# Linear attention beside a routed feed-forward layer: expert rows transposed on VectorE instead of TensorE, and three weight buffers

## The reference

```
xn  = layernorm(x)                        # x: [1, 1024, 256]
out = x + attention(xn) + ffn(xn)

attention: q, k, v = split(xn @ w_qkv);  q, k = elu(.) + 1;  16 heads of 16 columns
           s_t  = decay * s_{t-1} + k_t          # scan over the 1024 tokens
           kv_t = decay * kv_{t-1} + k_t * v_t
           (q * kv / max(sum_head(q * s), 1e-6)) @ w_out
ffn:       e(t), score(t) = the best of 8 experts by xn @ router_w.T
           routed = (silu(g) * u) @ w_down[e],   g, u = split(xn * sigmoid(score) @ w_gate_up[e])
           shared = (silu(g) * u) @ shared_down, g, u = split(xn @ shared_gate_up)
```

## Time and profile before

| | |
|---|---|
| median of 3 runs | 128.91 us (128.76 to 129.81) |
| the profiled execution's own time | 129.24 us |
| its span | 127.6 us |
| TensorE busy | 122.1 us (96%), clock granted in full |
| VectorE, ScalarE, GpSimd busy | 79.4 (62%), 53.4 (42%), 35.4 us (28%) |
| moved by DMA | 25.02 MB, mean 196 GB/s |

### The profile page before, as it was taken

How to read it: one execution, slowest core, us unless ns; L and a number is a source line. 1 busy time by engine, 2 the same in 40 slices (tenths; PEclk the granted TensorE clock), 3 DMA queues, 4 the chain that set the end, 5 groups by cost and what they waited for, 6 DMA issues and landing times.

```text
span 127.6 us, 2426 instructions
## 1 busy us (share of the span) xinstructions
PE 122.1 (96%) x822; PEld 106.1 (83%) x822; DVE 79.4 (62%) x175; ACT 53.4 (42%) x113; POOL 35.4 (28%) x65
## 2 busy tenths in 40 slices
PE   4989999999999999999999999999999999999990
PEld 1248776788888857999999999999999978999990
DVE  0799695997899999875575553505040428922471
ACT  1678796829987546322222222242221337200000
POOL 7804040003879300040303030303030301687500
PEclk9999999999999999999999999999999999999999
DMA  3784999999993210129797989888982031033437
GB/s 83 207 281 37 330 360 244 181 207 397 385 380 136 82 51 0 46 81 318 264 321 258 295 275 277 307 280 303 281 303 63 9 86 51 13 89 104 112 101 244
DMA packets 15748, 25.02 MB, mean 196 GB/s; under 512 B 1296, under 2 KB 12632, under 8 KB 15736
## 3 DMA queue, kind: packets, MB, share of 16 engines
q1 hardware_dynamic: 13368, 20.66, 53.1%
q0 software_dynamic: 1456, 3.41, 8.2%
q10 hardware_dynamic: 912, 0.80, 1.9%
HBM read 18.78 MB, written 6.08 MB: 195 GB/s over the span
## 4 chain that ended last, share of the span: by engine, by line
PE 80%; POOL 6%; issue 5%; DMA 4%; DVE 2%; ACT 0%; DVEq 0%; POOLq 0%
PE ps L1112 25%; PE ps L1126 13%; PE ps L300 6%; POOL q_sb L458 6%; PE ps L302 5%; PE ps L301 5%; PE ps L975 5%; PE ps L988 4%; PE ps L981 4%; PE ps L1066 4%; DMA q_sb<-sorted_rows,slot_row 2%; PE ps L1053 2%; DMA sorted_rows<-yrow 2%; PE ps L1060 2%; DVE x_sb L895 1%
## 5 line engine op out<-in xcount | busy, mean ns | idle before, releaser
L1112 PE MATMUL ps<-xgT,gu 128*128 128x144 f32 x256 | 34.2, 287 | 0.0
L1112 PEld LDWEIGHTS ps<-xgT,gu 128*128 128x128 f32 x256 | 32.3, 190 | 0.5 <-issue 0.2
L826 DVE TENSOR_TENSOR wqkv<-rz,ps 128x288 f32<-128x288 f32 x16 | 7.3, 454 | 25.5 <-ACT rz L576 25.5
L440 POOL DMA_DIRECT2D sorted_rows<-yrow x9 | 5.0, 558 | 54.7 <-DVE yrow L821 54.7
L1126 PE MATMUL ps<-wqkv,dn 128*128 128x144 f32 x128 | 17.4, 289 | 0.0
L576 ACT ACTIVATE rz<-ps 128x288 f32<-128x288 f32 x16 | 6.5, 409 | 25.0 <-PE ps L1112 25.0
L1126 PEld LDWEIGHTS ps<-wqkv,dn 128*128 128x128 f32 x128 | 16.1, 190 | 0.0
L432 POOL DMA_INDIRECT sorted_rows<-xn,slot_row x8 | 9.8, 1220 | 15.4 <-ACT xn L514 13.6
L300 PE MATMUL ps<-xT_hi,sgu_hi 128*128 128x512 f32 x32 | 13.0, 407 | 0.0
L301 PE MATMUL ps<-xT_lo,sgu_hi 128*128 128x512 f32 x32 | 12.6, 394 | 0.0
L302 PE MATMUL ps<-xT_hi,sgu_lo 128*128 128x512 f32 x32 | 12.6, 394 | 0.0
(11 more groups left out here) (162 smaller groups left out, 231.3 us busy)
## 6 DMA issues: line engine op xcount, KB each, us to landing
gu<-in_L_ffn_w_gate_up_dram SPq DMA_DIRECT2D x8, 1024.0 KB
dn<-in_L_ffn_w_down_dram SPq DMA_DIRECT2D x8, 512.0 KB
sorted_rows<-zeros SPq DMA_DIRECT2D x1, 2592.0 KB, 18.0
wqkv<-sorted_rows SPq DMA_DIRECT2D x10, 144.0 KB
sorted_rows<-yrow POOLq DMA_DIRECT2D x9, 128.0 KB, 2.1
sgu<-_ffn_shared_gate_up_dram SPq DMA_DIRECT2D x1, 1024.0 KB, 6.2
wqkv<-in_L_attn_w_qkv_dram SPq DMA_DIRECT2D x3, 256.0 KB, 3.7
x_sb<-in_L_attn_x_dram SPq DMA_DIRECT2D x2, 256.0 KB, 3.6
```

What stands on the lines that cost most here:

```text
L826: V.tensor_tensor(hr[:, 2 * h:2 * h + 2, :].rearrange("p f s -> p (f s)"), act_sb[:, h, 0:2 * SLOTS], ps[:, 2 * h + 1, 0:2 * SLOTS], ALU.m ...
L1112: ins = mm(ps[:, 2 * h + u, (f % 2) * SLOTS:(f % 2 + 1) * SLOTS], gu[p][:, kc, col:col + P], xgT[:, kc, :], start=(kc == 0), stop=(kc == K ...
```

## The change

- **Rows in.** The four DMAs of a new `sorted_load` each bring 32 partitions of `xg`: partition q*32 + p holds, for each of 5 blocks of 32 rows, 64 columns of row p of the block (256 bytes). One VectorE `transpose` of 32x32 blocks (`sorted_in`) makes `xgT` from it; TensorE's and ScalarE's part in this goes away. Features then lie in another order over the partitions, so `gu` is loaded as "(p c)" instead of "(c p)".
- **Results out.** `rows_out` transposes the down result from PSUM to `yrow` in one VectorE instruction; four DMAs store it, in the same pieces of 256 bytes, from SyncE's queue instead of GpSimd's. `yrow` has one buffer. For this order the down product takes every second column of `dn` as its weights. The last group's stores are issued two by SyncE and two by ScalarE.
- **Three weight buffers.** The third lies in `xT_raw` and `ez`, which are free once the routing and the q, k, v products are done. Expert 2 is loaded before the loop, and expert e + 3 after expert e.
- **Three parts.** Gate/up goes in parts of 2, 1 and 1 hidden blocks of 128 columns. The third part uses banks 4 and 7, which the transposes used before.
- **VectorE's list.** The first two `kv_scan` move from before the loop to after the first pass, the other two to after the second; the products with q move to after the fifth.

```diff
-        xg = early[0:HS, 0:2 * D].rearrange("p (j d) -> p j d", j=2)
+        gu_of = [gu[0][:, :, :], gu[1][:, :, :], xT_raw[:, :, :]]
+        dn_of = [dn[0][:, :, :], dn[1][:, :, :], ez[:, :, :].rearrange("p b t -> p (b t)").rearrange("p (f d) -> p f d", f=FC)]
+        xg = early[:, 0:NSQ * SQ * KC].rearrange("p (j f) -> p j f", j=NSQ)
...
-        gu_dram = w_gate_up.rearrange("e (c p) n -> e p c n", p=P)
+        gu_dram = w_gate_up.rearrange("e (p c) n -> e p c n", c=KC)
...
+        GATE = (0, 2, 4)
+        UP = (1, 3, 7)
+        PARTS = ((0, 1), (2,), (3,))
...
+        def row_store(eng, t, q, s_store):
+            rows = sorted_rows[bass.ds(t * SLOTS, NSQ * SQ), q * SQ * KC:(q + 1) * SQ * KC]
+            eng.dma_start(rows.rearrange("(j p) f -> p j f", p=SQ), yrow[q * SQ:(q + 1) * SQ, :, :]).then_inc(s_store, 16)
...
 # SyncE
+            def sorted_load(first, s_load):
+                for q in range(P // SQ):
+                    rows = sorted_rows[bass.ds(first, NSQ * SQ), q * SQ * KC:(q + 1) * SQ * KC]
+                    sp.dma_start(xg[q * SQ:(q + 1) * SQ, :, :], rows.rearrange("(j p) f -> p j f", p=SQ)).then_inc(s_load, 16)
...
                 with sp.Fori(ends[e - 1] if e else 0, ends[e]) as t:
-                    sp.wait_ge(s_xgT, t + 2)
-                    sorted_load(t + 2)
+                    sp.wait_ge(s_yrow, t + 1)
+                    for q in range(P // SQ):
+                        row_store(sp, t, q, s_ystore)
+                    sp.wait_ge(s_xgc, t + 2)
+                    sorted_load(t * SLOTS + 3 * SLOTS, s_xg)
...
 # refill: after pass e, expert e + 3 (was e + 2)
+                sp.wait_ge(s_gup, 3 * done)
+                sp.dma_start(gu_of[p][:, :, :], gu_dram[e + 3]).then_inc(s_gu[p], 16)
                 sp.wait_ge(s_down, done)
+                sp.dma_start(dn_of[p][:, :, :], dn_dram[e + 3]).then_inc(s_dn[p], 16)
...
+            sorted_load(SLOTS, s_xg0)
+            sp.wait_ge(s_lrow, 1)
+            sp.wait_ge(s_q, 2 * NH)
+            expert_load(2)
...
 # ScalarE
             def expert_tile(t):
-                for h in range(2):
-                    act.wait_ge(s_gup, 2 * t + (h + 1))
-                    A(act_sb[:, h, 0:2 * SLOTS], ps[:, 2 * h, 0:2 * SLOTS], ACT.Silu).then_inc(s_silu, 1)
-                sorted_copy(t + 2, 4)
-                act.wait_ge(s_down, t + 1)
-                A(yT[:, 0:KC * P].rearrange("p (c s) -> p c s", c=KC), ps[:, 5:7, 0:P], ACT.Copy)
-                A(yT[:, KC * P:].rearrange("p (s c) -> p c s", c=KC), ps[:, 5:7, P:SLOTS], ACT.Copy).then_inc(s_yT, 1)
+                for h in range(3):
+                    act.wait_ge(s_gup, 3 * t + (h + 1))
+                    A(silu_part(h), ps[:, GATE[h], 0:len(PARTS[h]) * SLOTS], ACT.Silu).then_inc(s_silu, 1)
...
 # VectorE
+            def sorted_in():
+                V.transpose(xgT[:, :, :], xg.rearrange("p j (f c) -> p c j f", c=KC)).then_inc(s_xgc, 1)
...
+            def rows_out(t, s_done):
+                dve.wait_ge(s_down, t)
+                dve.wait_ge(s_ystore, 64 * t)
+                V.transpose(yrow[:, :, :].rearrange("p j (f c) -> p c j f", c=KC), ps[:, 5:7, 0:NSQ * SQ]).then_inc(s_done, 1)
...
+            def expert_tile(t, first=False):
+                if not first:
+                    rows_out(t, s_yrow)
+                expert_part(t, 0)
+                expert_part(t, 1)
+                dve.wait_ge(s_xg, 64 * t + 64)
+                dve.wait_ge(s_gup, 3 * t + 3)
+                sorted_in()
+                expert_part(t, 2)
...
 # TensorE, in a pass
-                        if h == 0:
-                            pe.wait_ge(s_yrow, t + 1)
-                            transpose_back(t + 1)
-                    transpose_sorted(4, s_xg, 16 * t + 16)
-                    pe.wait_ge(s_dn[p], 16 * (e // 2) + 16)
-                    for h in range(2):
-                        pe.wait_ge(s_hr, 2 * t + (h + 1))
+                    pe.wait_ge(s_yrow, t + 1)
+                    pe.wait_ge(s_dn[p], 16 * (e // 3) + 16)
+                    for h in range(3):
+                        pe.wait_ge(s_hr, 3 * t + (h + 1))
                         for c in range(KC):
-                            for f in (2 * h, 2 * h + 1):
-                                ins = mm(ps[:, 5 + c, 0:SLOTS], dn[p][:, f, c * P:(c + 1) * P], hr[:, f, :],
+                            for f in PARTS[h]:
+                                ins = mm(ps[:, 5 + c, 0:SLOTS], dn_of[p][:, f, :].rearrange("p (m c) -> p c m", c=KC)[:, c, :], hr[:, f, :],
                                          start=(f == 0), stop=(f == FC - 1))
```

More of the change, by code:

```diff
@@ L190, in build @@
         s_sdn = sem("s_sdn")
-        s_gu = [sem(f"s_gu{p}") for p in range(2)]
-        s_dn = [sem(f"s_dn{p}") for p in range(2)]
+        s_gu = [sem(f"s_gu{p}") for p in range(3)]
+        s_dn = [sem(f"s_dn{p}") for p in range(3)]
         s_zero = sem("s_zero")
@@ L266, in build @@
         s_down = sem("s_down")
-        s_yT = sem("s_yT")
-        s_yback = sem("s_yback")
         s_yrow = sem("s_yrow")
[L270 to L273, removed]
+        s_ystore = sem("s_ystore")
+        s_lastrow = sem("s_lastrow")
+        s_ylast_sp = sem("s_ylast_sp")
+        s_ylast_act = sem("s_ylast_act")
         s_gather = [sem(f"s_gather{i}") for i in range(NT)]
@@ L359, in _ @@
             sp.wait_ge(s_wlq, 1)
[L360 removed]
+            sorted_load(SLOTS, s_xg0)
+            sp.wait_ge(s_lrow, 1)
+            sp.wait_ge(s_q, 2 * NH)
+            expert_load(2)
             sp.wait_ge(s_plan, 1)
[L363 to L365 removed]
+            sp.wait_ge(s_xgc, 1)
+            sorted_load(2 * SLOTS, s_xg)
+            for e in range(E - 3):
                 refill(e)
[L367 removed]
+            for e in range(E - 3, E):
                 rows_of(e)
[L369 to L371 removed]
+            sp.wait_ge(s_xg, 64 * ends[7] + 64)
+            sp.wait_ge(s_lastrow, 1)
+            for q in range(2):
+                row_store(sp, ends[7], q, s_ylast_sp)
             for i in range(1, NT, 2):
@@ L597, in attention_hi @@
                 A(att_hi[:, c, cols], kvsum[:, c, cols], ACT.Copy).then_inc(s_atth, 1)
+            act.wait_ge(s_lastrow, 1)
+            for q in range(2, P // SQ):
+                row_store(act, total, q, s_ylast_act)
             attention_hi(0)
@@ L1100, in _ @@
             for e in range(E):
-                p = e % 2
-                pe.wait_ge(s_gu[p], 16 * (e // 2) + 16)
+                p = e % 3
+                pe.wait_ge(s_gu[p], 16 * (e // 3) + 16)
                 with pe.Fori(ends[e - 1] if e else 0, ends[e]) as t:
                     pe.wait_ge(s_xgc, t + 1)
-                    for h in range(2):
-                        if e == 0 and h == 1:
+                    for h in range(3):
+                        if e == 0 and h == 2:
                             pe.wait_ge(s_denc, 1)
+                            pe.wait_ge(s_sh, LAST)
```

161 lines of the change are left out of this document (51 added, 110 removed).

## The result

The changed kernel takes 127.54 us median (126.29 to 128.33, 4 runs) against 129.08 us for the kernel before (128.76 to 129.81, 4 runs): ratio 0.9842 (95% interval 0.98 to 0.9884), 2.0 us faster. Forecast were 124.4 us and a gain of 4.6. The profiled execution took 126.29 us and has a span of 124.2; it is the shortest of the four.

A forecast was written before the change was run, and what follows sets the result against it. TensorE, busy 96% of the span and 80% of the chain, was taken as the bound; 5.2 us of transposes + 0.2 at the tail - 0.8 of queue waits = 4.6 us gained, giving 124.4 us, range 123.0 to 129.0.

The forecast's parts named there:

- Transposes off TensorE: TensorE in the loop, the shared tile and between shared products: removing its transposes saves 5.2 us, 4.64 of it in the loop.
- Strided weight loads: Down product on TensorE: reading every second column as weights costs 0, since loads hide behind products; high bound 16 us.
- VectorE's transposes: VectorE, two block transposes a pass: 0.47 us for 320 elements, bounds 0.40 and 0.94.
- rival 1: Transposed rows or third part come late on VectorE, costing 0.3 us a pass, 2.4 us: 126.8 us; chance 0.19 with more queue wait.
- The moved scans: VectorE work moved after part 2 of a pass: worst 3.4 us, ending before down needs its results; cost 0.
- The tail: After the loop: 0.33 us of transposes go, gathers start 4.4 us after the loop and additions follow TensorE, 0.2 us more gained.
- A 256-byte piece: DMA row loads and stores: 28 ns a piece, between 10 and 54, so 1280 pieces take 2.3 us of all engines a pass.
- Rival 2: DMA queue becomes the bound and the kernel slower: 132 us at 45 ns a piece, 136 at 54; chance 0.10 of slower.
- the sign named for being wrong: DMA row pieces: the forecast is wrong if a 256-byte piece takes over 38 ns, where the 4.6 us gain is used up.
- The engines' work in a refilling pass: DMA engines: 2.3 us of row pieces and 4.2 of weights make 6.5 us, over the 5.93 us pass by 0.6.
- The waits: Loop, row stores queued behind weights: only the last two refilling passes are late, 0.4 us each, 0.8 us lost.
- by 2.9: Row store must land by 2.9 us into the next pass, since the single result buffer may be rewritten only then.

## Why the prediction was right in direction and wrong in size

- **Transposes off TensorE, 5.2 us (4.64 in the loop, 0.25 ahead of it, 0.33 behind): right, a little low.** The loop ran 50.73 to 103.27 before, 52.5 us; without waits it is 47.19, 5.35 us less, and it begins 0.5 us sooner. A pass without waits is 5.88 us for 5.93.
- **Strided weight loads, 0: right.** The chain has sixteen down records in 1.96 us, 123 ns from one to the next, where it had 2.01 and 126 before. The Trainium skill (SBUF — State Buffer, Door 1: The DMA port swizzle) has full rate while two accesses share a 16-byte line; the trace agrees.
- **VectorE's transposes, 0.47 us: 0.52.** In the first passes, where no store is late, down follows gate/up without a gap: rival 1 did not occur. The moved scans cost nothing.
- **The tail, 0.5 us (0.33 of transposes, 0.2 of gathers): 0.3.** From the loop's end to the end of the span it is 24.0 us (before 24.3). The first gather came at 106.24, 6.05 us after the loop and not 4.4, since SyncE's last stores stood behind the wait for the useless row load and left at 103.28.
- **A 256-byte piece, 28 ns: high.** Row loads alone (548 packets between 44.0 and 46.5, share 0.22) give 0.22 x 2.5 x 16 / 548 = 16 ns, last stores alone (373 between 103.2 and 105.8, share 0.21) 23 ns. Rival 2's ground, dear pieces, was not there, and stores in 1280-byte pieces gained nothing; the sign named for being wrong, over 38 ns a piece, stayed silent, and the forecast failed all the same. The Trainium skill (DMA: Bandwidth & Descriptors, Specifications) wants 512 bytes or more for full rate; here 256-byte pieces moved 256/16 = 16 GB/s an engine against 418/16 = 26 for weights, so the rate does fall, and for the stores no time of the kernel hung on it.
- **The engines' work in a refilling pass, 6.5 us: about right, from two errors that offset each other.** Length times busy share comes to 38.3 us over the eight passes and to 16.1 without refills, so a refill costs 4.4 us (forecast 4.2) and the rows of a pass 1.8 (forecast 2.3): 6.2 us.
- **The waits, 0.8 us: this step failed.** It read: "A store issued at 0.7 to 2.2 of a pass [...] lands some 1.2 us after its turn, near 2 into the next pass: 1 us to spare [...] So the last two refilling passes are late, 0.4 us each: 0.8 us." The profiled execution has 2.8 us of waits, and the medians with and without refills differ by 4.1. The work in the engines was priced well enough; the step from it to the waits was not. Two sizes in it were wrong. First, "10 x 0.38 = 3.8 us of 5.93: it fits": a row DMA costs SyncE 0.53 us with the steps to the next one (4.26 us for eight), and the whole list is 6.02. SyncE itself had no room, so the stores leave late and the refill 2.2 us into the next pass. Second, the landing: I had the weights in front of a store stream at once, and they start some 2 us after issue. In the pass from 68.21 the store leaves at 72.13, 3.9 us in, and lands at 77.93, 3.6 us into the pass from 74.38, where "by 2.9" was the last moment.
- **Outside the span, 0.** The profiled execution before was 1.6 us longer than its span, that of the changed kernel 2.1: 0.5 us given back that no step had. The same 2.1 holds without refills, and 1.8 with the refills on GpSimd; the cause is open.

So on the span: 0.5 + 5.35 + 0.3 - 2.8 = 3.4 us (127.6 to 124.2), less 0.5 outside it: 2.95 for the profiled execution, and about 1 less in a usual run. The forecast's terms without waits made 5.4 us and came to 6.2, which by luck hid 0.8 of the 2.0 us that the waits were short.

**What is settled:** the refills cause the waits (none without them). It is not the stores' piece size, the scans or VectorE's speed. SyncE's list, the ring of the stores and the work of the DMA engines (5.9 to 6.8 us) are all near or over a pass. Neither a shorter list (stores from GpSimd, one store DMA, refills from GpSimd) nor a queue without weights ends the waits, and a second buffer, another order or the refills on GpSimd move them to the row loads. **What is open:** how much of the 4 us belongs to the list, to the landing and to full engines, since leaving out refills lowers all three at once; and why a refill needs about 2 us to run at speed.

## What to carry to other kernels

When a step is moved to a queue, add up that engine's whole list in a pass with the times between issues, not only the issues: here 3.8 us on paper were 6.0. When a single buffer is freed by a DMA, follow the ring from landing to landing under the heaviest traffic, not at the landing time of a quiet stretch (1.6 us against 3.5 to 5), and compare it with the pass; a second buffer was the cheapest help found. Read the engines' busy share pass by pass too. When a wait goes, look for the next transfer that stands behind the same bytes. And before an experiment's time is put down to its waits, look at the granted clock after them.

## What the runs showed of the hardware that was not expected

- A 40 KB DMA lands in 1.6 to 1.8 us (median) without refills. In the passes that wait, beside 1.5 MB of weights, the last of four takes 3.5 to 5.0 us on the weights' queue, 3.3 to 4.7 from GpSimd's, and on SyncE's queue with the weights on another engine's 4.7 to 5.9 (loads) and 5.6 to 7.0 (stores).
- Leaving out 0.5 MB of down took most of the waits away, leaving out 0.5 MB of gate/up little. The first also takes a DMA from SyncE's list.
- In a wait of 3.5 us TensorE's granted clock fell from 1.00 to 0.50 (refills behind the stores), and the 32 gate/up records behind it took 6.26 us instead of 4.08. In the changed kernel, whose longest wait is 1.1 us, it stayed at 1.00.
